# A recommendation model's pair products: 13 block copies within SBUF in place of a round trip through memory, and one sample per matmul

## What is computed

```python
bot_out = _mlp(dense_x, [bw0, bw1, bw2], [bb0, bb1, bb2])
gathered = jnp.stack([emb[t][sparse_x[:, t]] for t in range(emb.shape[0])], axis=1)
...
features = jnp.concatenate([bot_out[:, None, :], gathered], axis=1)
Z = jnp.einsum('bnd,bmd->bnm', features, features)
interact = Z[:, LI, LJ]
x = jnp.concatenate([bot_out, interact], axis=1)
return _mlp(x, [tw0, tw1, tw2, tw3, tw4], [tb0, tb1, tb2, tb3, tb4])
```

## Time and profile before

| | |
|---|---|
| median of 3 runs | 180.82 us |
| span of the profiled execution | 179.6 us |
| time outside the span, against that median | 1.2 us |
| TensorE busy | 167.0 us, 93% |
| VectorE, ScalarE, GpSimd busy | 46%, 37%, 56% |
| rows through the gather queue, through SP's queue | 6.82 MB, 12.89 MB |

### The profile page before, as it was taken

The page is one execution under the profiler, slowest core; times in us unless marked ns, Lnnn a source line. Parts: engine busy times, 40 slices in busy tenths (PEclk is TensorE's granted clock), DMA queues, the critical chain, the costliest instruction groups (busy, mean ns, idle before and its releaser), DMA issues.

```text
span 179.6 us, 3315 instructions
## 1 busy us (share of the span) xinstructions
PE 167.0 (93%) x1354; PEld 128.6 (72%) x1354; DVE 82.2 (46%) x177; ACT 66.3 (37%) x103; POOL 100.7 (56%) x112
## 2 busy tenths in 40 slices
PE   1999999899599994999999999989999999999993
PEld 1335557568377783798878889977888898788992
DVE  3202588955165756374452346343506625411422
ACT  0576748664143655133033253112504611110211
POOL 3777776777777777777777777767772000000000
PEclk9999999999999999799999999999999999999999
DMA  4999972434499733242232244422223120000000
GB/s 97 369 337 391 390 239 58 100 66 89 89 302 374 285 79 86 54 100 68 44 61 51 52 105 85 93 46 62 46 59 72 24 53 7 4 0 0 0 0 4
DMA packets 10124, 19.93 MB, mean 111 GB/s; under 512 B 5639, under 2 KB 5771, under 8 KB 9981
## 3 DMA queue, kind: packets, MB, share of 16 engines
q1 hardware_dynamic: 6636, 12.89, 22.0%
q0 software_dynamic: 3328, 6.82, 16.7%
q10 hardware_dynamic: 144, 0.00, 0.0%
HBM read 18.26 MB, written 1.44 MB: 110 GB/s over the span
## 4 chain that ended last, share of the span: by engine, by line
PE 71%; DMA 10%; POOL 8%; issue 4%; SPq 2%; DVE 2%; ACT 2%; POOLq 0%; DVEq 0%; ACTq 0%
PE acc L799 14%; PE acc L803 13%; PE acc L800 12%; POOL rows L420 8%; PE feat L781 6%; PE turned L944 5%; PE feat L763 5%; DMA rows<-in_emb,index 3%; PE turned L881 3%; DMA pairs<-pair_scratch 3%; DMA pair_scratch<-dots 3%; PE acc L829 2%; PE acc L938 2%; PE feat L938 2%; DMA v<-in_bw 1%
## 5 line engine op out<-in xcount | busy, mean ns | idle before, releaser
L420 POOL DMA_INDIRECT rows<-in_emb,index x104 | 99.5, 957 | 34.4 <-issue 30.0
L799 PE MATMUL acc<-w1h,y_split 128*128 128x512 f32 x64 | 27.9, 436 | 0.0
L803 PE MATMUL acc<-w1h,y_split 128*128 128x512 f32 x64 | 26.1, 407 | 0.0
L800 PE MATMUL acc<-w1l,y_split 128*128 128x512 f32 x64 | 25.5, 399 | 0.0
L444 ACT COPY featT<-feat 128x512 f32<-128x512 f32 x16 | 17.6, 1097 | 14.4 <-PE feat L763 14.3
L457 ACT ACTIVATE y_split<-turned 128x512 fp32r<-128x512 f32 x16 | 9.7, 606 | 35.1 <-PE turned L881 35.1
L651 DVE SCALAR_TENSOR_TENSOR y_split<-turned,y_split 128x512 fp32r<-128x512 f32 x16 | 11.1, 692 | 18.7 <-ACT y_split L457 18.7
L799 PE MATMUL acc<-w2h,y_split 128*128 128x256 f32 x64 | 18.8, 294 | 0.0
L803 PE MATMUL acc<-w2h,y_split 128*128 128x256 f32 x64 | 18.0, 281 | 0.0
L763 PE MATMUL feat<-ident,rows 128*128 128x128 f32 x104 | 15.3, 277 | 2.7 <-DMA rows<-in_emb,index 2.7
L800 PE MATMUL acc<-w2l,y_split 128*128 128x256 f32 x64 | 17.8, 279 | 0.0
(11 more groups left out here) (107 smaller groups left out, 255.6 us busy)
## 6 DMA issues: line engine op xcount, KB each, us to landing
w1r<-in_w SPq DMA_DIRECT2D x8, 512.0 KB, 13.8
w2r<-in_w SPq DMA_DIRECT2D x4, 512.0 KB, 6.0
rows<-in_emb,index POOLq DMA_INDIRECT x104, 3.0
w0r<-in_w_pairs SPq DMA_DIRECT2D x3, 512.0 KB, 7.8
top<-in_top_rows SPq DMA_DIRECT2D x1, 1024.0 KB, 12.1
pair_scratch<-dots SPq DMA_DIRECT2D x8, 104.0 KB, 2.3
pair_scratch<-dots SPq DMA_DIRECT2D x8, 71.5 KB
v<-in_bw SPq DMA_DIRECT2D x1, 512.0 KB, 3.6
```

Of the source, the lines that this page charges most:

```text
L420: pool.indirect_dma_start(rows[:, i, :], None, table, bass.IndirectOffsetOnAxis(ap=index[:, c, i:i + 1], axis=0)).then_inc(s_gather[LOTS * ...
L799: nc.tensor.matmul(dst, ah, wh, start=first, stop=False)
L800: nc.tensor.matmul(dst, ah, wl, start=False, stop=False)
L803: return nc.tensor.matmul(dst, al, wh, start=False, stop=end)
```

## The change

The scratch tensor in memory is gone. `dots` keeps all 27 columns instead of 26. The pairs are covered by 13 rectangular blocks of (features n0 to n0+ns) by (features m0 to m0+ms); each is one transfer from `dots` to `pairs`, within SBUF. A block of ns features lies on ns partitions of `dots` and goes to ns*ms partitions of `pairs`, 256 bytes each. Blocks that hold a pair twice or a square have zero weights in its second place (`pair_weights`, on the host). Tile 0 takes 1 transfer (126 rows), tile 1 takes 7 (117 rows), tile 2 takes 5 (127 rows and the bias row). Every half uses one sample per matmul.

```diff
+BLOCKS = (
+    ((14, 9, 0, 14),),
+    ((7, 7, 0, 7), (18, 5, 14, 4), (4, 3, 0, 4), (11, 3, 7, 4), (5, 2, 4, 2), (12, 2, 11, 2), (19, 4, 18, 4)),
+    ((0, 24, 23, 4), (24, 2, 25, 2), (1, 3, 0, 3), (8, 3, 7, 3), (15, 3, 14, 3)),
+)
+PAIR_ROWS = [sum(n * m for _, n, _, m in blocks) for blocks in BLOCKS]
+TILE_ROWS = [PAIR_ROWS[0], PAIR_ROWS[1], PAIR_ROWS[2] + 1]
+PINS = [16 * len(blocks) for blocks in BLOCKS]
...
-        dots = sb("dots", [P, COLS, HALF])
+        dots = sb("dots", [P, FEATS, HALF])
...
-            def scratch_out(c, h):
+            def pairs_back(c, h):
 
                 sp.wait_ge(s_za, HALVES * c + h + 1)
                 sp.wait_ge(s_zd, HALVES * c + h + 1)
-                for i in range(PAIR_TILES):
-                    after(sp, s_pin[h][i], (16 if i < PAIR_TILES - 1 else 32) * c)
-                low, mid = HALF * h, HALF * h + FIRST_ROWS
-                sp.dma_start(scratch[h, 0:FIRST_ROWS], dots[low:mid]).then_inc(s_scr0[h], 16)
-                sp.dma_start(scratch[h, FIRST_ROWS:], dots[mid:low + FEATS]).then_inc(s_scr1[h], 16)
...
                 after(sp, s_xlp, PAIR_TILES * c)
                 if (c, h) == (0, 0):
                     sp.wait_ge(s_one, 1)
-                sp.wait_ge(s_scr0[h], 16 * (c + 1))
-                sp.dma_start(pairs[0:PAIR_ROWS, 0, half], pairs_of(h, 0, TILE_FEATS)).then_inc(s_pin[h][0], 16)
-                sp.wait_ge(s_scr1[h], 16 * (c + 1))
-                sp.dma_start(pairs[0:PAIR_ROWS, 1, half],
-                             pairs_of(h, TILE_FEATS, TILE_FEATS)).then_inc(s_pin[h][1], 16)
...
+                for i, blocks in enumerate(BLOCKS):
+                    row = 0
+                    for n0, ns, m0, ms in blocks:
+                        sp.dma_start(pairs[row:row + ns * ms, i, h * HALF:(h + 1) * HALF],
+                                     dots[HALF * h + n0:HALF * h + n0 + ns, m0:m0 + ms, :]).then_inc(s_pin[h][i], 16)
+                        row += ns * ms
...
             def dots_out(c, h):
 
-                after(act, s_scr0[h], 16 * c)
-                after(act, s_scr1[h], 16 * c)
+                for i in range(PAIR_TILES):
+                    after(act, s_pin[h][i], PINS[i] * c)
...
-                    act.wait_ge(s_pin[h][i], (16 if i < PAIR_TILES - 1 else 32) * (c + 1))
+                    act.wait_ge(s_pin[h][i], PINS[i] * (c + 1))
                 after(act, s_l[0], 2 * c)
-                nc.scalar.copy(xh[0:PAIR_ROWS + 1, i, :], pairs[0:PAIR_ROWS + 1, i, :]).then_inc(s_xhp, 1)
+                nc.scalar.copy(xh[0:TILE_ROWS[i], i, :], pairs[0:TILE_ROWS[i], i, :]).then_inc(s_xhp, 1)
...
-                (sample_pairs if half < HALVES * CHUNKS - 1 else single_samples)(h)
-
-            def sample_pairs(h):
-
-                for g in range(GROUPS):
-                    for q in range(0, QUADS, 2):
...
-            def single_samples(h):
-
                 for g in range(GROUPS):
                     for q in range(QUADS):
                         sample = featT[:, h, QUADS * g + q, 0:FEATS]
```

More of the change, by code:

```diff
@@ L52 @@
 SMALL = 8
-def pair_order():
-    tiles = []
-    for i in range(PAIR_TILES):
[L63 to L72, removed]
 def pair_weights(w, bias):
     out = np.zeros((PAIR_TILES, P, w.shape[1]), w.dtype)
-    for at, (a, b) in enumerate(pair_order()):
-        out[at // PAIR_ROWS, at % PAIR_ROWS] = w[DIM + a * (a - 1) // 2 + b]
-    out[PAIR_TILES - 1, PAIR_ROWS] = bias
+    placed = set()
+    for i, blocks in enumerate(BLOCKS):
+        row = 0
+        for n0, ns, m0, ms in blocks:
+            for n in range(n0, n0 + ns):
+                for m in range(m0, m0 + ms):
+                    a, b = max(n, m), min(n, m)
+                    if a != b and (a, b) not in placed:
+                        placed.add((a, b))
+                        out[i, row] = w[DIM + a * (a - 1) // 2 + b]
+                    row += 1
+    assert len(placed) == FEATS * (FEATS - 1) // 2
+    out[PAIR_TILES - 1, PAIR_ROWS[PAIR_TILES - 1]] = bias
     return out
@@ L98, in after, with rec_kernel @@
         eng.wait_ge(sem, count)
-def rec_kernel(nc, x_turned, sparse, emb, bw, small, w0_bot, w0_pairs, w1, w2, w3_in, top_rows, scratch, out):
+def rec_kernel(nc, x_turned, sparse, emb, bw, small, w0_bot, w0_pairs, w1, w2, w3_in, top_rows, out):
     with ExitStack() as ctx:
@@ L265, in dot_quadrant @@
             block_ = feat[QUAD * q:QUAD * q + FEATS, :].rearrange("n (g c) -> n c g", c=GROUP_COLS)
-            return dots[HALF * h:HALF * h + FEATS, :, at:at + GROUPS], block_[:, q * FEATS:q * FEATS + COLS, :]
+            return dots[HALF * h:HALF * h + FEATS, :, at:at + GROUPS], block_[:, q * FEATS:(q + 1) * FEATS, :]
         FIRST_PACED = 36
@@ L616, in dots_out @@
             def dots_out(c, h):
-                after(dve, s_scr0[h], 16 * c)
-                after(dve, s_scr1[h], 16 * c)
+                for i in range(PAIR_TILES):
+                    after(dve, s_pin[h][i], PINS[i] * c)
                 dve.wait_ge(s_z, HALVES * c + h + 1)
@@ L772, in dots_of @@
                 pe.wait_ge(s_fb, half + 1)
-                (sample_pairs if half < HALVES * CHUNKS - 1 else single_samples)(h)
-            def sample_pairs(h):
-                for g in range(GROUPS):
-                    for q in range(0, QUADS, 2):
-                        samples = featT[:, h, QUADS * g + q:QUADS * g + q + 2, :]
-                        at = g * GROUP_COLS + q * FEATS
-                        ins = nc.tensor.matmul(
-                            feat[QUAD * q:QUAD * q + PAIR_COLS, at:at + 2 * FEATS].rearrange("n (s m) -> n s m", s=2),
-                            samples.rearrange("d s n -> d (s n)")[:, 0:PAIR_COLS], samples[:, :, 0:FEATS],
-                            start=True, stop=True)
-                ins.then_inc(s_z, 1)
-            def single_samples(h):
                 for g in range(GROUPS):
@@ L838, in layer0 @@
                 lo_ready = (s_xlp, PAIR_TILES * c + k + 1) if half == 0 else None
-                n = PAIR_ROWS + (k == PAIR_TILES - 1)
+                n = TILE_ROWS[k]
                 cols = slice(half * NB, (half + 1) * NB)
@@ L1087 @@
                aps["in_small"], aps["in_w0_bot"], aps["in_w0_pairs"], aps["in_w1"], aps["in_w2"], aps["in_w3"],
-               aps["in_top_rows"], scratch, out)
+               aps["in_top_rows"], out)
     result = run(nc, [arrays], core_ids=[0])
```

23 lines of the change are left out of this document (3 added, 20 removed).

## The result

The changed kernel takes **210.71 us** (median of 4 runs, 210.33 to 211.04) against 180.96 for the kernel before beside it: a ratio of 1.163, 95% interval 1.158 to 1.169. It is 16% slower. The forecast was 180.4, the range 179.2 to 184.2, so the result lies far outside it. The profiled span is 208.9 us, 29.3 more than before.

A forecast was written before the change was run, and what follows sets the result against it. TensorE and POOL's gather stream were taken to run at the same pace, tied in a ring. A net shift of -0.4 us took the span from 179.6 to 179.2; plus 1.2 outside it, 180.4 us, range 179.2 to 184.2.

The forecast's parts named there:

- Step 3: Four reads from memory become 13 copies issued by SP, ten short at 0.33 us; 5.44 us to the last start.
- L: Time from SP's first issue to tile 2 landed: forecast 7.4 us, bounds 6.3 and 9.3, against 7.08 before.
- Step 4: Following L = 7.4 through chunks 1 to 3: tile 2 shifts +0.04, -0.90 and -0.4 us, the last being the total.
- the ring: Loop of gathers, dots, transfers, tile 2 rounding and layer 0 releasing a gather; past L = 7.5, 3 us per us.
- Rival C: TensorE's clock drops to 1.2 GHz around longer gaps before tile 2: +1.3 us, 181.7 for one drop; chance 0.03.
- Step 1: One sample per matmul: dots -0.67 us in each of 7 halves, transfers starting 0.59 us sooner in those halves.
- Rival D: Single-sample matmuls run at the double ones' pace, 0.061 us each, 3.9 us a half: about 188 us; chance 0.02.
- Step 2: SP's two writes to memory and the wait for them go: 2.40 us off each half.
- Rival B: SP's issue train sets the end, short copies 0.45 to 0.49 us each: 183.8 us at L = 8.6; chance 0.29.

The follow-up runs named there:

- e7: Changed kernel with only eight of its 13 copies, one sample per matmul, 45 rows left out: 186.17 us, 1.029 of the kernel before.
- e5: Changed kernel without the gather's wait on layer 0: 211.51 us, 1.166 of the kernel before.
- e6: Changed kernel with only the three large copies and two samples per matmul: 179.62 us, 0.994 of the kernel before.

## Why the prediction was wrong

**Step 3 failed, and it carries the result.** The ten short copies were charged 0.33 us each, with 0.49 as the upper bound. They took 0.65 to 0.78; the three large ones 0.85, 0.82 and 0.83 against 0.79, 0.52 and 0.68. Up to the start of the last copy that is 9.38 us against 5.44; the landing was 1.80 against 1.96; so L = 11.2 (11.6 in chunk 1) where the forecast had 7.4 and its far bound 9.3 (the terms named for it add up to 9.45). The working went wrong at the choice of rows: every row has memory on one side, and the working took what 13 rows cost for the ceiling of a short one and one row written to the output, 0.24, for its floor. That row's form is a write to memory from one partition. A copy from SBUF to SBUF has its own price, 0.55 in the cheapest form tried. Where the trace has no row of the operation, the upper bound has to reach at least to the dearest issue in sight: 0.77 was in the same group, and with 0.77 for the ten L comes to 11.4.

**Step 4, the ring, named the right pieces and made them too short.** The ring's own formula at L = 11.2, with everything else as written, gives +3.8, +6.7 and +10.7 in chunks 1 to 3, about 191.5 us. So the mis-sized term explains some 11 us through the formula, and e7 shows the ring too short at the forecast's own L. Piece by piece, the 29.3 us of the profile are 13.7 of longer trains in chunks 1 to 3, 6.2 between the dots and SP's first transfer, 4.5 that chunk 0 handed on, 3.1 between the rounding and the next dots, and 1.8 in the tail. What the formula left out:
- Chunk 0 was to be absorbed by TensorE's idle wait before 71.69. It was 5.7 us late and only 1.2 was absorbed, because the gather that layer 0 releases in chunk 0 had no slack. Without that wait a later gather, which waits for TensorE's transposes, idled POOL for 5.11 us before 61.70 (e5). POOL's timeline, before and after:

```profile
50.91 0.95 POOL L420 DMA_INDIRECT rows<-in_emb,index  x1 [0.30 <-PE acc L803]
```

```profile
57.83 1.08 POOL L393 DMA_INDIRECT rows<-in_emb,index  x1 [4.99 <-PE acc L761]
```

- The first half's train was taken to be out of the way. In chunk 2 the second half's dots were copied at 124.57 and SP came free at 125.13, 0.5 us later; in chunk 3 they were copied at 163.50 and SP came free at 166.01, 2.5 later.
- **Rival C happened in every chunk**, not once: 0.7 us each in chunks 1 and 2 from the rounding to the release. Of the 0.9 us more from there to the dots the clock can hold most: it was still at 1.2 GHz at 99.6, 1.4 us after the gather at 98.25, and half of that is 0.7 (an estimate).
- Step 1's two savings did not come, as told next.

**Step 1 failed in sign.** The -0.67 in each of seven halves and the 0.59 sooner start came from the last half's 1.27 us, the one half in which no gather runs. With gathers 64 matmuls take 1.7 to 3.2 us in the changed kernel. The row was right, but it was carried from a stretch without gathers to seven with them. Rival D thus named the right place, at 0.02, with a fixed pace as its reason; the pace was not fixed, 20 ns a matmul without gathers (1.27 us) and 49 in the slowest half with them (3.15).

The Trainium skill (TensorE: Matmul & The Clock Gate, section "Wait — 56ns, not 53.3ns?") gives about 62 ns per matmul with hardware decode switched off. By that figure 64 would take 4.0 us, an estimate. Which way it is set here no run shows, but at 20 ns a matmul where no gather ran the figure isn't what binds.

**Step 2 was right.** The two writes and their wait of 2.40 us are gone, and three copies without them, with two samples per matmul, are 1.2 us faster than before (e6).

**Rival B was the right mechanism**: the issue train sets the end, tile 2 waits in all four chunks. It was priced at 183.8 for L = 8.6, and about +5 at L = 9.3, by the same too low bound, and the slope beyond L = 7.6 was given as 3 us per us of L. Between e7 and the changed kernel, whose L differ by 3.0 to 4.0, it was 24.5 us, 6 to 8 us per us: chunk 0, the blocked second trains and the clock come in as well, and no run takes these apart.

That the bytes don't matter held, since 3 GB/s moved while the core waited. What failed first were the two prices, both taken from rows of another kind of transfer or of another load.

## What to carry to other kernels

Count transfers, not rows, when regrouping within SBUF: here each copy took 0.55 to 0.88 us of its queue however small, so the round trip with its six issues (7.1 us until the last tile was rounded) beat 13 direct copies (11.2), and a second queue won only part of it back. Three copies with two samples per matmul beat both and eight copies with one did not, but neither carries all the pairs. Take the price of a small matmul from a stretch that is as loaded with gathers as the place where it will run, and ask of a ring whether each wait that should absorb a delay has slack in its own trigger.

## What the runs showed that was not expected

- A copy of one 256-byte row from SBUF to SBUF took SP 0.55 us, one of 126 rows 0.85 to 0.88; one of 16 plain rows from memory 0.42. 27 rows from 27 partitions cost 0.18 more than 16 from 16.
- With one sample per matmul the same kernel took 215.0 us in a marked job and 182.3 in another, on the same chip; without the gathers of chunks 2 and 3 it took 193.8 and 177.7. So of the 32.7 us between the two, 16.5 go with half of the gathers: a good part of the slowness of those jobs comes where gathers run.
- TensorE was granted 1.2 GHz in each of the four holes of the changed kernel, in which it was idle for 4.7 to 6.5 us, and had the full clock back 3 to 4 us after it had begun to work again. A gap of 1.8 us in chunk 2 of e7 left it full.
